# Taking a softmax's exponential in quarters of a row tile, 1536 columns at a time, on one NeuronCore

## The reference

```python
anchor_adj = jnp.einsum('md,de,ne->mn', x, weight, input)      # 6144 x 6144
scores = jnp.where(adj > 0, anchor_adj, NEG_PAD)
atten = jax.nn.softmax(scores / 0.07, axis=1)
x = layernorm(x + atten @ input)
# layer 1: e = leaky_relu(s1[:,None] + s2[None,:]) from Wh = x @ W
att = softmax(where(adj > 0, e, NEG_INF), axis=1)
x = layernorm(x + elu(att @ Wh))
```

## Time and profile before

| | us |
|---|---|
| runs of the kernel | 1686.52, 1684.52, 1681.19 (median 1684.52) |
| span of the profiled execution, first to last instruction | 1683.9 |
| TensorE busy / VectorE busy / ScalarE busy in it | 1604.5 / 1499.4 / 863.7 |
| granted TensorE clock, share of full speed | 0.982 |

### The profile page before, as it was taken

How to read it: one execution, slowest core, us unless ns; L and a number is a source line. 1 busy time by engine, 2 the same in 40 slices (tenths; PEclk the granted TensorE clock), 3 DMA queues, 4 the chain that set the end, 5 groups by cost and what they waited for, 6 DMA issues and landing times.

```text
span 1683.9 us, 41477 instructions
## 1 busy us (share of the span) xinstructions
PE 1604.5 (95%) x13614; PEld 1340.3 (80%) x13614; DVE 1499.4 (89%) x3368; ACT 863.7 (51%) x2111; POOL 430.8 (26%) x330
## 2 busy tenths in 40 slices
PE   6899989998998998999999899999999999999996
PEld 3577767776776776776777677789999999999996
DVE  6999979997997997998899799978999999999996
ACT  3577767776776775777677677784000000000000
POOL 5322322332332332322233222300222222222210
PEclk9899999999999999999999999999999999999998
DMA  7756664665665666566566566546676677667772
GB/s 239 254 204 228 229 219 174 232 232 189 226 222 179 232 232 225 178 228 222 195 233 232 167 221 232 218 92 114 140 156 151 145 150 156 145 148 155 157 149 40
DMA packets 380440, 317.43 MB, mean 189 GB/s; under 512 B 306240, under 2 KB 331072, under 8 KB 380224
## 3 DMA queue, kind: packets, MB, share of 16 engines
q1 hardware_dynamic: 380224, 314.75, 61.3%
HBM read 160.56 MB, written 78.64 MB: 142 GB/s over the span
## 4 chain that ended last, share of the span: by engine, by line
PE 87%; issue 6%; DVE 4%; ACT 1%; DVEq 0%; POOL 0%; POOLq 0%; ACTq 0%
PE ps L559 28%; PE ps L488 15%; PE ps L464 14%; PE ps L466 7%; PE ps L498 7%; PE ps L500 7%; PE ps L499 7%; DVE pT_lo L738 1%; DVE rows L729 1%; DVE adj_sb L901 1%; PE ps L530 0%; ACT rows L625 0%; ACT pT_hi L619 0%; PE ps L422 0%; PE ps L537 0%
## 5 line engine op out<-in xcount | busy, mean ns | idle before, releaser
L559 PE MATMUL ps<-rows,adj_sb 128*128 128x129 f32 x4608 | 518.2, 275 | 1.4 <-DVE adj_sb L901 1.4
L559 PEld LDWEIGHTS ps<-rows,adj_sb 128*128 128x128 f32 x4608 | 517.1, 192 | 1.6 <-issue 1.6
L901 DVE SCALAR_TENSOR_TENSOR adj_sb<-rows,late,edge_sb 128x512 f32<-128x512 f32 (+1 forms) x576 | 440.6, 796 | 45.3 <-PE ps L559 17.7
L619 ACT CAST pT_hi<-ps 128x512 f16<-128x512 f32 x576 | 337.6, 586 | 253.7 <-PE ps L488 246.7
L729 DVE CUSTOM_DVE_ANT_0 rows<-ps,edge_sb 128x512 f32<-128x512 f32 x576 | 394.9, 686 | 66.7 <-issue 30.2
L464 PE MATMUL ps<-vals,pT_hi 128*128 128x256 f16 x2304 | 446.6, 274 | 0.9 <-ACT att L613 0.8
L625 ACT ACTIVATE rows<-rows,exp_bias 128x512 f32<-128x512 f32 x576 | 417.3, 725 | 21.8 <-DVE exp_bias L792 21.8
L738 DVE TENSOR_TENSOR pT_lo<-ps,pT_hi 128x512 f16<-128x512 f32 x576 | 394.8, 685 | 29.5 <-issue 23.6
L350 POOL TENSOR_SCALAR edge_sb<-edge_sb 128x1536 bf16<-128x1536 bf16 x192 | 283.0, 1474 | 534.0 <-DVE edge_sb L706 533.9
L466 PE MATMUL ps<-vals,pT_lo 128*128 128x128 f16 x2304 | 414.9, 220 | 0.0
L488 PE MATMUL ps<-ident,rows 128*128 128x128 f32 x2304 | 355.3, 277 | 40.9 <-DVE pT_lo L738 38.3
(11 more groups left out here) (99 smaller groups left out, 734.7 us busy)
## 6 DMA issues: line engine op xcount, KB each, us to landing
adj_sb<-adj SPq DMA_DIRECT2D x192, 768.0 KB, 7.3
edge_rows<-edge_sb SPq DMA_DIRECT2D x192, 384.0 KB, 7.3
rows<-inp SPq DMA_DIRECT2D x4, 768.0 KB, 9.3
xq<-x SPq DMA_DIRECT2D x48, 64.0 KB, 2.0
xr<-x SPq DMA_DIRECT2D x48, 64.0 KB, 1.8
out<-vals SPq DMA_DIRECT2D x12, 256.0 KB, 2.7
edge_sb<-edge_rows SPq DMA_TRANSPOSE x96, 5.5
x1T<-w SPq DMA_DIRECT2D x1, 64.0 KB, 1.8
```

The source lines that it names most:

```text
L559: mm = nc.tensor.matmul(ps[:, 4 * par + k, 0:P + 1], p1_slot(n)[:, k * P:(k + 1) * P], vals1[:, n, 0:P + 1], start=(n == 0), stop=(n == NB ...
L619: nc.scalar.copy(pT_hi[:, bc % PT_SLOTS, :], ps[:, PT0 + bc % NPT, :]).then_inc(pT_hi_set, 1)
L901: nc.vector.scalar_tensor_tensor(out=p1_slot(n), in0=r_all[:, bass.ds(g * CHUNK, CHUNK)], scalar=col_of[:, E_OF, n:n + 1], in1=edgesT[:, p ...
```

## The change

The exponential is issued at c = 0, 3, 6 and 9 only, each time over the 1536 columns of a quarter, with one accumulated sum each. `part_sum` shrinks to four columns for each parity. TensorE's wait before a transpose counts quarters in place of chunks, and so does VectorE's wait ahead of `exp_bias`.

```diff
-        part_sum = sb("part_sum", [P, 2, C], F32)
+        part_sum = sb("part_sum", [P, 2, QUARTERS], F32)
...
+        def row_quarter(par, q):
+            return rows[:, par * N + q * QW:par * N + (q + 1) * QW]
...
-                        pe.wait_ge(exp_set, C * (t - off) + bc + 1)
+                        pe.wait_ge(exp_set, QUARTERS * (t - off) + bc // QC + 1)
...
-                        nc.scalar.activation(row_chunk(1 - par, c), row_chunk(1 - par, c), ACT.Exp,
-                                             bias=exp_bias[:, 1 - par:2 - par], scale=EXP_SCALE,
-                                             accum_out=part_sum[:, 1 - par, c:c + 1]).then_inc(exp_set, 1)
+                        if c % QC == 0:
+                            nc.scalar.activation(row_quarter(1 - par, c // QC), row_quarter(1 - par, c // QC), ACT.Exp,
+                                                 bias=exp_bias[:, 1 - par:2 - par], scale=EXP_SCALE,
+                                                 accum_out=part_sum[:, 1 - par, c // QC:c // QC + 1]).then_inc(exp_set, 1)
...
-                        after(dve, exp_set, C * (t - 1) if known is None or known >= 2 else 0)
+                        after(dve, exp_set, QUARTERS * (t - 1) if known is None or known >= 2 else 0)
```

## The result

Over 18 runs each on one chip the changed kernel takes 1689.32 us and the kernel before 1681.49 us (medians): ratio 1.0048, 95% interval 1.0035 to 1.0061. It is slower by 7.8 us or 0.5%. The time lies inside the stated range and 3.3 us above the 1686.0 us forecast, but the change is five times the +1.5 us of the sum, and more than the 5.1 us up to which I had counted a change as none. Its runs scatter from 1681.67 to 1696.63, those of the kernel before from 1678.26 to 1686.52. The profiled execution took 1687.3 us with a span of 1685.5, so 1.8 us lie around the span.

What follows compares the result with a forecast made beforehand. TensorE was taken to set the pace at 1.75 us a step. Zero for steady tiles, tile 1 and back edges plus 1.5 us for tile 48, on 1684.5 us, gave 1686.0 us; range 1680 to 1691.

Steps and rivals of the forecast that it cites:

- the sum: Whole kernel: steady tiles, tile 1 and back edges 0 each, tile 48 +1.5 us, added to a 1684.5 us median.
- The wide exponential's price: ScalarE in layer 0: one exponential over 1536 columns takes 1.58 us, from 0.834 ns a column.
- Steady tiles at 0: Layer 0's steady row tiles: TensorE's 21.39 us covers ScalarE's saving and the late copies, so 0 us.
- The late copy: ScalarE's copy behind a wide exponential, steps 4, 7, 10: 0.36 us late, 0.42 us of VectorE's cover left in step 7.
- Rival (a): Steady tiles: late copy stalls VectorE if the wide exponential holds ScalarE over 2.05 us; about 9 us slower, 1695 us; chance 0.08.
- Rival (c): Tile 48: its two-bank ring does not bind, so ScalarE's saving counts, -2.4 us, 1682.1 us; chance 0.06.
- Tile 48 at +1.5 us: Layer 0's last tile, where ScalarE leads: copies delayed into a two-bank ring, +1.5 us, bounds -2.4 and +2.3.
- TensorE's wait for the exponential and tile 1: Transposes come three steps after the wide exponential, so 0; in tile 1 a later VectorE wait absorbs it, at most 0.85 us.
- Back edges at 0: Six jumps of the tile loop: VectorE's stall is in its own program, ScalarE's first copy comes early, so 0 us.
- rival (b), "longer": Loop back edges: VectorE's stalls lengthen instead of shortening; no size given, chance 0.06.
- The sign that I had set for it: Back edges: prediction wrong if idle time at the six edges moved by more than 5 us in sum.

Runs made afterwards that it cites:

- e4: Changed kernel with the loop over tiles written out, so no engine branches in layer 0: 1626.71 us, ratio 0.9658 to the kernel before.
- e10: Loop over tiles written out, wide exponentials except narrow ones in the last row tile: 1625.59 us, ratio 0.9647 to the kernel before.
- e3: Kernel before (narrow exponentials) with the loop over tiles written out: 1626.19 us, ratio 0.9653 to the kernel before.
- e2: Changed kernel with twelve narrow exponentials in the last row tile only: 1687.77 us, ratio 1.0016 to the kernel before.
- e1: Changed kernel run again without edit: 1689.32 us against 1684.81 for the kernel before, ratio 1.0026.
- e5: Changed kernel, each wide exponential adding 3 to its semaphore, so TensorE's and VectorE's programs are as before: 1690.41 us, ratio 1.0045 to the kernel before.
- e6: Changed kernel with two long-satisfied waits added to ScalarE's program in steps without an exponential: 1687.53 us, ratio 1.0023 to the kernel before.
- e12: Kernel before with twelve tiny copies put once into VectorE's program ahead of the loop: 1651.85 us, ratio 0.9808 to the kernel before.
- e8: Changed kernel with twelve tiny copies put once into VectorE's program ahead of the loop: 1656.00 us, ratio 0.9837 to the kernel before.
- e9: Changed kernel with five long-satisfied waits ahead of SyncE's second adjacency load of each loop tile: 1688.44 us, ratio 1.0014 to the kernel before.
- e11: Changed kernel with twenty long-satisfied waits ahead of SyncE's second adjacency load of each loop tile: 1688.06 us, ratio 1.0023 to the kernel before.

## Why the prediction was right or wrong

- **The wide exponential's price: right.** 1.58 us forecast, 1578 ns measured; the slope from two unlike exponentials held for the third. ScalarE's 125 us lie within the 100 to 140 forecast.
- **Steady tiles at 0: right.** 21.35 us a tile in both kernels. The late copy was 0.3 us late (0.36 forecast), with 0.50 us left (0.42). Rival (a) never came near its 2.05 us: the wide exponential holds ScalarE for 1.57 us. Rival (c), that ScalarE's saved time counts, is refuted: tile 48 became longer, and e4 and e10 gain nothing clear on e3.
- **Tile 48 at +1.5 us: right, measured +1.77.** The quarter's second copy starts 1.57 us after the exponential and the next quarter's first 2.10 us after that, as worked out from the earlier trace rows. e2 undoes it alone.
- **TensorE's wait for the exponential and tile 1: right.** From bias to bias the first tiles take 19.98 and 21.12 us in both profiles.
- **Back edges at 0: this is the step that failed.** I argued that VectorE's program is unchanged and ScalarE's copy early, which is so (VectorE's jump has the same number of instructions ahead of it, and the first copy is out at 244.74 before L742 at 253.71). But a stall behind an unchanged jump is not of unchanged length: in the two profiles of the kernel before alone the second stall went from 2.04 to 4.40 us, and the three runs that I had could not bound it. The term that I put at 0 came to 2.7 to 6.0 us (the 4.5 and 7.8 us between the medians of the unaltered kernels, less 1.8 for tile 48). Over the profiles the six edges sum to 181.5 us (two of the kernel before) and to 185.0 us (five of the wide form: changed, e1, e2, e5, e6), 3.5 us more; with 1.8 us from tile 48 that makes 5.3, between the 4.5 us of e1 and the 7.8 us of the first chip. One kernel's edge sums differ by 2 to 4 us between two profiles, so this sum alone would be weak; with the edges gone most of the difference goes too (e3, e4: 0.5 us), and that places it. Of the 4.2 us between e12 and e8 (on two chips), 1.8 are tile 48 and 1.7 the first stalls (edges 149.3 and 151.0); with one profile each, that is an indication. This was rival (b), "longer", to which I gave 0.06. The sign that I had set for it, idle time at the six edges moved by more than 5 us in sum, did not show: from the first profile of the kernel before, 47.1 us, it moved by 1.3 us in the changed kernel and by 3.2 in e1. It was set too coarse for one pair of profiles.
- **The size of the noise, and luck.** I took 5.1 us as what a measurement can tell. Eighteen runs a side told 7.8 us from 0 with an interval of some 2 us on either side; from the first set of runs to that of e1 the ratio moved from 1.0048 to 1.0026. My sum started from three runs with a median of 1684.52 us, and eighteen gave 1681.49. That start, 3 us too high, hid half of what the sum lacked: from 1681.5 the sum would have said 1683.0 us, 6.3 under the 1689.32 measured. So that the time came out 3.3 us from the forecast is in part luck.

What stays open is why the wide form makes the edges longer. It is not TensorE's program (e5). ScalarE's is not ruled out, since e6 gave back half of its length and not the time at which its packets leave. Shorter edges go with a late SyncE load, in these traces; moving that load by hand did not clearly bring the time back (e9, e11), so it is a correlation and not shown as the cause. The Trainium skill, Runtime: NRT & Kernel Launch, section "Instruction fetch mechanics", says that a jump out of the pages held has to wait for a DMA of its target. e3 and e8 agree with it: no jump, no stall; a target placed elsewhere, one stall in place of two. That e8 was a matter of the target's place in a block of the program I conclude from the stall's vanishing; the blocks' borders are not in the trace, and no run tried a number of copies that should leave the second stall in place.

## What to carry to other kernels

Here an engine that was third in a stage gave nothing back when its instructions were merged, and merging cost 1.77 us where it led. Before merging, ask in which stretch it leads, and how deep the ring is that its output passes through; there a coarse instruction delays what stands behind it. Look for idle time that no semaphore explains at the back edges of a hardware loop: here six of them held 55 us, 3.3% of the kernel, seven times what the change was worth, and writing the loop out took them away. Where it can't be written out, try moving the loop's first instruction with a few cheap ones ahead of it, and look again at whether an engine stalls once or twice.

## What the runs showed of the hardware

- A back edge cost 8.6 to 9.2 us in the kernel before (edge tiles of 29.9 and 30.6 us on average in its two profiles, less 21.35), and 3.5 to 3.8 us in the shifted loops (149.3 and 151.0 us for six, e12 and e8).
- Twelve copies of one column, run once, saved 28 to 32 us (e8, e12).
- Behind an idle time of 6.21 us TensorE was granted 0.50 of its clock for 3.2 us (kernel before, first edge); behind the single stall of e8 and of e12 at that edge it had 1.00.
- A DMA issue on SyncE, usually 0.33 us, took 0.51 to 0.66 us at eleven of the 18 edges of the kernel before (two profiles) and of e12; at each of them the 8 KB program packet that I take for ScalarE's had started up to 0.1 us before the bias, and so 0.15 to 0.22 us before the issue. At four more edges with such a packet it took 0.33 to 0.40 us.
